# Attention output bias: from a TensorE product per tile to a GpSimd addition behind the first norm

## The reference, cut to what matters

```
for each batch:
  xa = layernorm(x)                        # norm "A"
  x  = x + (attention(q = xa@Wq.T + bq, k = ctx@Wk.T + bk, v = ctx@Wv.T + bv) @ Wo.T + bo)
  x  = x + mixture(layernorm(x))           # norm "R": top-3 of 12 experts, 2 stages of 12 matrices, gelu between
  x  = x + attention(layernorm(x), ctx, ctx)   # norm "C": no projections
  x  = x + moe(layernorm(x))               # norm "D": router over 64 experts, shared expert, routed experts
```

## Time and profile before

| | |
|---|---|
| median of 3 runs | 2767.86 us |
| the profiled execution | 2765.2 us, its span 2763.4 us |
| TensorE (PE) busy | 2616.3 us, 95% of the span |
| VectorE (DVE) busy | 2207.7 us, 80% |
| ScalarE (ACT) busy | 1067.6 us, 39% |
| GpSimd (POOL) busy | 811.1 us, 29% |
| chain that ended last | PE 77%, DVE 12%, issue 4% |

### The profile page before, as it was taken

The page is one execution under the profiler, slowest core; times in us unless marked ns, Lnnn a source line. Parts: engine busy times, 40 slices in busy tenths (PEclk is TensorE's granted clock), DMA queues, the critical chain, the costliest instruction groups (busy, mean ns, idle before and its releaser), DMA issues.

```text
span 2763.4 us, 59981 instructions
## 1 busy us (share of the span) xinstructions
PE 2616.3 (95%) x22949; PEld 2189.8 (79%) x22949; DVE 2207.7 (80%) x6135; ACT 1067.6 (39%) x1622; POOL 811.1 (29%) x829
## 2 busy tenths in 40 slices
PE   3899999999999999999999999999999999985999
PEld 3778788888888888888888888888888888863776
DVE  5677888888888888888888888888888888762554
ACT  3333434444444444433444444444444344322332
POOL 1000133322323232322332232323232232226444
PEclk9999999999999999999999999999999999986999
DMA  7644444444444444443444444444344333245997
GB/s 226 174 141 107 114 127 129 124 109 115 118 118 110 117 112 97 117 118 93 107 112 99 107 117 112 109 112 113 89 106 109 93 98 83 55 87 157 230 234 169
DMA packets 322210, 336.02 MB, mean 122 GB/s; under 512 B 46676, under 2 KB 302751, under 8 KB 321412
## 3 DMA queue, kind: packets, MB, share of 16 engines
q1 hardware_dynamic: 286404, 307.37, 42.8%
q0 software_dynamic: 33792, 18.52, 4.0%
q10 hardware_dynamic: 1728, 6.29, 0.7%
HBM read 191.65 MB, written 221.81 MB: 150 GB/s over the span
## 4 chain that ended last, share of the span: by engine, by line
PE 77%; DVE 12%; issue 4%; DMA 2%; ACT 2%; POOL 2%; SPq 1%; POOLq 0%; ACTq 0%; DVEq 0%
PE mixp L1386 35%; PE attn_out L1320 6%; PE second L1304 5%; DVE nm L978 4%; PE first L1286 4%; DVE hid L1070 3%; PE misc L1254 3%; PE misc L1212 3%; PE mixp L1488 3%; PE misc L1422 2%; PE misc L1331 2%; PE second L1507 2%; PE misc L1461 2%; PE misc L1350 2%; PE first L1443 2%
## 5 line engine op out<-in xcount | busy, mean ns | idle before, releaser
L793 ACT ACTIVATE exps<-second 128x1024 f32<-128x1024 f32 x512 | 525.4, 1026 | 770.9 <-PE second L1304 763.6
L678 POOL DMA_INDIRECT expert_slots<-row_mem,sidx x512 | 510.4, 997 | 820.1 <-PE first L1286 579.1
L1386 PE MATMUL mixp<-w_h,r_part_h 128*128 128x256 f32 x3072 | 664.2, 297 | 2.3 <-DVE r_part_l L888 1.1
L978 DVE TENSOR_REDUCE nm<-first 128x4 f32<-128x1024 f32 x504 | 614.3, 1219 | 24.8 <-PE first L1286 24.2
L1386 PE MATMUL mixp<-w_h,r_part_l 128*128 128x256 f32 x3072 | 609.8, 280 | 0.0
L1386 PE MATMUL mixp<-w_l,r_part_h 128*128 128x256 f32 x3072 | 609.3, 279 | 0.0
L1386 PEld LDWEIGHTS mixp<-w_h,r_part_h 128*128 128x128 f32 x3072 | 467.8, 189 | 43.4 <-issue 2.1
L1386 PEld LDWEIGHTS mixp<-w_l,r_part_h 128*128 128x128 f32 x3072 | 468.8, 188 | 0.0
L1386 PEld LDWEIGHTS mixp<-w_h,r_part_l 128*128 128x128 f32 x3072 | 468.6, 188 | 0.0
L1070 DVE SCALAR_TENSOR_TENSOR x_mem<-mixp,C,x_mem 128x256 f32<-128x256 f32 x768 | 332.6, 477 | 74.5 <-PE mixp L1386 67.5
L1070 DVE SCALAR_TENSOR_TENSOR hid<-mixp,C,hid 128x256 f32<-128x256 f32 x704 | 303.6, 477 | 54.4 <-PE mixp L1386 52.9
(11 more groups left out here) (236 smaller groups left out, 3593.1 us busy)
## 6 DMA issues: line engine op xcount, KB each, us to landing
kst<-k_parts SPq DMA_DIRECT2D x256, 192.0 KB, 4.1
qst<-q_parts SPq DMA_DIRECT2D x256, 192.0 KB, 4.5
q_parts<-nat_h SPq DMA_DIRECT2D x128, 256.0 KB
k_parts<-ctx_part_h SPq DMA_DIRECT2D x64, 256.0 KB, 2.5
k_parts<-nat_h SPq DMA_DIRECT2D x64, 256.0 KB, 5.6
q_parts<-nat_l SPq DMA_DIRECT2D x64, 256.0 KB
exps<-in_wgu SPq DMA_DIRECT2D x30, 384.0 KB, 4.2
expert_slots<-row_mem SPq DMA_DIRECT2D x16, 642.0 KB, 6.5
```

The lines of the kernel that those rows point to most:

```text
L678: pool.e.indirect_dma_start(out=slots_dram, out_offset=bass.IndirectOffsetOnAxis(ap=sidx[b % 2][:, t, k:k + 1], axis=0), in_=row[b % 2][:, ...
L793: act.e.activation(exps[:, j % NU, :, :, :].rearrange("p k t s -> p (k t s)"), second[:, :, :].rearrange("p k s -> p (k s)"), ACT.Exp, sca ...
L978: dve.e.tensor_reduce(nm[u % 2][:, :, 2 * j:2 * j + 2].rearrange("p t k -> p k t"), (mixp_mem if in_mixp(b, kind, j) else first)[:, :, :]. ...
L1386: m = pe.e.matmul(mixp[q % 2][:, t * D:(t + 1) * D], src[i][:, dt, t * P:(t + 1) * P], wmix[n][j][:, l, dt, :], start=(k == 0), stop=(k == ...
```

## The change

GpSimd adds the bias, and all strings are written anew. The parts:

1. At the start TensorE makes one product of `ones` with the whole of `b_rows` (line 1238 of the new kernel), once, and ScalarE copies it into a new tile `bias` (128 x 256): the bias row in each partition. (The rows from 32 on of `ones` are zero, so that b2 does not enter.)
2. A new GpSimd step e of norm A: after VectorE has normalised x of the batch, GpSimd adds `bias` to both tiles of X in one instruction and raises `p_bias`.
3. Step m on TensorE has no bias product, and m on VectorE also waits for `p_bias`.
4. `pw` and `b2_raw`, read only at the start, move into `out_sb`, whose first other write waits for both splits. Semaphore `p_id` becomes the first count of `p_const`.
5. All five strings of `ORDERS` change: GpSimd's by 32 letters e, the others only in order.

```diff
+        bias = sb("bias", (P, D))
-        b_raw = out_sb[0:2, 0, :]
+        b_raw, pw, b2_raw = out_sb[0:2, 0, :], out_sb[0:64, 1, :], out_sb[B2, 1, :]
...
+                elif what == "ln2" and a[0] == "A":
+                    _, b = a
+                    pool.wait_ge(v_norm["A"], 2 * b + 2)
+                    pool.wait_ge(a_b, 3)
+                    pool.e.tensor_tensor(X[b % NXB][:, :, :], X[b % NXB][:, :, :],
+                                         bias[:, :].unsqueeze(1).broadcast_to([P, TILES, D]), ALU.add).then_inc(p_bias, 1)
...
             for c in range(FIRST):
                 load_chunk(2 * FIRST + c)
+            act.wait_ge(t_bo, 2)
+            act.e.copy(bias[:, :], misc[:, 0:D]).then_inc(a_b, 1)
...
                 elif what == "o_proj":
                     b, = a
                     dve.wait_ge(t_o, b + 1)
+                    dve.wait_ge(p_bias, b + 1)
...
             pe.wait_ge(a_id, 1)
+            pe.wait_ge(v_g, 1)
+            pe.wait_ge(v_b, 2)
+            pe.e.matmul(misc[:, 0:D], ones[:, :].broadcast_to([P, P]), b_rows[:, :], start=True, stop=True).then_inc(t_bo, 1)
+            free["misc"] = [(a_b, 3)]
...
                     pe.wait_ge(v_w, 1)
-                    pe.wait_ge(v_b, 1)
                     for t in range(TILES):
                         out = misc[:, t * D:(t + 1) * D]
-                        pe.e.matmul(out, ones[:, :].broadcast_to([P, P]), b_rows[:, :], start=True, stop=False)
                         for i, j in TERMS:
                             for dt in range(DT):
-                                m = pe.e.matmul(out, a_parts[i][:, dt, t * P:(t + 1) * P], wo[j][:, dt, :], start=False,
-                                                stop=(i, j, dt) == (0, 1, DT - 1))
+                                m = pe.e.matmul(out, a_parts[i][:, dt, t * P:(t + 1) * P], wo[j][:, dt, :],
+                                                start=(i, j, dt) == (0, 0, 0), stop=(i, j, dt) == (0, 1, DT - 1))
```

More of the change, by code:

```diff
@@ new lines @@
+        "OTOTOTwcCTDOOTOTdOTOOTOTeTOTOTOTBOTOTTnOOTOTOTwcCTOOTDOTdOTOOTOTeTOTOTOTBOTOTTnOOTOTOTwcCTOOTDOTdOTOOTOTeTOTOT"
+        "OTBOTOTTnOOTOTOTwcCTOOTDOTdOTOOTOTeTOTOTOTBOTOTTnOOTOTOTwcCTOOTDOTdOTOOTOTeTOTOTOTBOTOTTnOOTOTOTwcCTOOTDOTdOTO"
+        "OTOTeTOTOTOTBOTOTTnOOTOTOTwcCTOOTDOTdOTOOTOTeTOTOTOTBOTOTTnOOTOTOTwcCTOOTDOTdOTOOTOTeTOTOTOTBOTOTTnOOTOTOTwcCT"
+        "OOTDOTdOTOOTOTeTOTOTOTBOTOTTnOOTOTOTwcCTOOTDOTdOTOOTOTeTOTOTOTBOTOTTnOOTOTOTwcCTOOTDOTdOTOOTOTeTOTOTOTBOTOTTnO"
+        "OTOTOTwcCTOOTDOTdOTOOTOTeTOTOTOTBOTOTTnOOTOTOTwcCTOOTDOTdOTOOTOTeTOTOTOTBOTOTTnOOTOTOTwcCTOOTDOTdOTOOTOTeTOTOT"
@@ new lines @@
+        "OTBOTOTTnOOTOTOTwcCTOOTDOTdOTOOTOTeTOTOTOTBOTOTTnOOTOTOTwcCTOOTDOTdOTOOTOTeTOTOTOTBOTOTTnOOTOTOTwcCTOOTDOTdOTO"
+        "OTOTeTOTOTOTBOTOTTnOOTOTOTwcCTOOTDOTdOTOOTOTeTOTOTOTBOTOTTnOOTOTOTwcCTOOTDOTdOTOOTOTeTOTOTOTBOTOTTnOOTOTOTwcCT"
+        "OOTDOTdOTOOTOTeTOTOTOTBOTOTTnOOTOTOTwcCTOOTDOTdOTOOTOTeTOTOTOTBOTOTTnOOTOTOTwcCTOOTDOTdOTOOTOTeTOTOTOTBOTOTTnO"
+        "OTOTOTwcCTOOTDOTdOTOOTOTeTOTOTOTBOTOTTnOOTOTOTwcCTOOTDOTdOTOOTOTeTOTOTOTBOTOTTnOOTOTOTwcCTOOTDOTdOTOOTOTeTOTOT"
+        "OTBOTOTTnOOTOTOTwcCTOOTDOTdOTOOTOTeTOTOTOTBOTOTTnOTOOTOTwCOTOTDOOTTOOTOTTOTOTOTBOTOTnTTwTTCTDOOTOOTTOTTOTTOTTT"
@@ new lines @@
+        "QtPfQQsRRvFPQGQhKQRRiQlQQPQRRQpQQPRRrckQtyQQQFPfQGQsRRvQQhKPRRiQlQQQRRPQQpQQPRRrckQtQyQQFPfQGQsRRvQQhKRRPiQQlQ"
+        "QPRRQQpQQPRRrckQtQyQQFPfQGQsRRvQQhKRRPiQQlQQPRRQQpQQPRRrckQtQyQQFPfQGQsRRvQQhKRRPiQQlQQPRRQQpQQPRRrckQtQyQQFPf"
+        "QGQsRRvQQhKRRPiQQlQQPRRQQpQQPRRrckQtQyQQFPfQGQsRRvQQhKRRPiQQlQQPRRQQpQQPRRrckQtQyQQFPfQGQsRRvQQhKRRPiQQlQQPRRQ"
+        "QpQQPRRrckQtQyQQFPfQGQsRRvQQhKRRPiQQlQQPRRQQpQQPRRrckQtQyQQFPfQGQsRRvQQhKRRPiQQlQQPRRQQpQQPRRrckQtQyQQFPfQGQsR"
+        "RvQQhKRRPiQQlQQPRRQQpQQPRRrckQtQyQQFPfQGQsRRvQQhKRRPiQQlQQPRRQQpQQPRRrckQtQyQQFPfQGQsRRvQQhKRRPiQQlQQPRRQQpQQP"
@@ new lines @@
+        "RRrckQtQyQQFPfQGQsRRvQQhKRRPiQQlQQPRRQQpQQPRRrckQtQyQQFPfQGQsRRvQQhKRRPiQQlQQPRRQQpQQPRRrckQtQyQQFPfQGQsRRvQQh"
+        "KRRPiQQlQQPRRQQpQQPRRrckQtQyQQFPfQGQsRRvQQhKRRPiQQlQQPRRQQpQQPRRrckQtQyQQFPfQGQsRRvQQhKRRPiQQlQQPRRQQpQQPRRrck"
+        "QtQyQQFPfQGQsRRvQQhKRRPiQQlQQPRRQQpQQPRRrckQtQyQQFPfQGQsRRvQQhKRRPiQQlQQPRRQQpQQPRRrckQtQyQQFPfQGQsRRvQQhKRRPi"
+        "QQlQQPRRQQpQQPRRrckQtQyQQFPfQGQsRRvQQhKRRPiQQlQQPRRQQpQQPRRrckQtQyQQFPfQGQsRRvQQhKRRPiQQlQQPRRQQpQQPRRrckQtQyQ"
+        "QFPfQGQsRRvQQhKRRPiQQlQQPRRQQpQQPRRrckQtQyQQFPfQGQsRRvQQhKRRPiQQlQQPRRQQpQQPRRrckQtQyQQFPfQGQsRRvQQhKRRPiQQlQQ"
@@ new lines @@
+        "LOoOSMOpOqPwrMMOxSMOyMMDMMOEuMOPMdMfOGMMOJevOSMOhMPHMMiSOMMOlMOmOPnMIMLMOoOSMMOpOqPrMwMOxSMOMyMMDMOEuMOPMdMfOG"
+        "MMOeJvOSMhOMPHMMiOSMMOlMOmOPnSMMIMOLoOMMOpOqPrMwMOSxMOMyMDMMEOuMOPMdMfOGMMOeJvOSMhOMPMHMiOSMMOlMOmOPnSMIMMOLoO"
+        "MMOpOqPrMwMOSxMOMyMDMMEOuMOPMdMfOGMMOeJvOSMhOMPMHMiOSMMOlMOmOPnSMIMMOLoOMMOpOqPrMwMOSxMOMyMDMMEOuMOPMdMfOGMMOe"
+        "JvOSMhOMPMHMiOSMMOlMOmOPnSMIMMOLoOMMOpOqPrMwMOSxMOMyMDMMEOuMOPMdMfOGMMOeJvOSMhOMPMHMiOSMMOlMOmOPnSMIMMOLoOMMOp"
+        "OqPrMwMOSxMOMyMDMMEOuMOPMdMfOGMMOeJvOSMhOMPMHMiOSMMOlMOmOPnSMIMMOLoOMMOpOqPrMwMOSxMOMyMDMMEOuMOPMdMfOGMMOeJvOS"
@@ new lines @@
+        "MhOMPMHMiOSMMOlMOmOPnSMIMMOLoOMMOpOqPrMwMOSxMOMyMDMMEOuMOPMdMfOGMMOeJvOSMhOMPMHMiOSMMOlMOmOPnSMIMMOLoOMMOpOqPr"
+        "MwMOSxMOMyMDMMEOuMOPMdMfOGMMOeJvOSMhOMPMHMiOSMMOlMOmOPnSMIMMOLoOMMOpOqPrMwMOSxMOMyMDMMEOuMOPMdMfOGMMOeJvOSMhOM"
+        "PMHMiOSMMOlMOmOPnSMIMMOLoOMMOpOqPrMwMOSxMOMyMDMMEOuMOPMdMfOGMMOeJvOSMhOMPMHMiOSMMOlMOmOPnSMIMMOLoOMMOpOqPrMwMO"
+        "SxMOMyMDMMEOuMOPMdMfOGMMOeJvOSMhOMPMHMiOSMMOlMOmOPnSMIMMOLoOMMOpOqPrMwMOSxMOMyMDMMEOuMOPMdMfOGMMOeJvOSMhOMPMHM"
+        "iOSMMOlMOmOPnSMIMMOLoOMMOpOqPrMwMOSxMOMyMDMMEOuMOPMdMfOGMMOeJvOSMhOMPMHMiOSMMOlMOmOPnSMIMMOLoOMMOpOqPrMwMOSxMO"
@@ new lines @@
+        "MyMDMMEOuMOPMdMfOGMMOeJvOSMhOMPMHMiOSMMOlMOmOPnSMIMMOLoOMMOpOqPrMwMOSxMOMyMDMMEOuMOPMdMfOGMMOeJvOSMhOMPMHMiOSM"
+        "MOlMOmOPnSMIMMOLoOMMOpOqPrMwMOSxMOMyMDMMEOuMOPMdMfOGMMOeJvOSMhOMPMHMiOSMMOlMOmOPnSMIMMOLoOMMOpOqPrMwMOSxMOMyMD"
+        "MMEOuMOPMdMfOGMMOeJvOSMhOMPMHMiOSMMOlMOmOPnSMIMMOLoOMMOpOqPrMwMOSxMOMyMDMMEOuMOPMdMfOGMMOeJvOSMhOMPMHMiOSMMOlM"
+        "OmOPnSMIMMOLoOMMOpOqPrMwMOSxMOMyMDMMEOuMOPMdMfOGMMOeJvOSMhOMPMHMiOSMMOlMOmOPnSMIMMOLoOMMOpOqPrMwMOSxMOMyMDMMEO"
+        "uMOPMdMfOGMMOeJvOSMhOMPMHMiOSMMOlMOmOPnSMIMMOLoOMMOpOqPrMwMOSxMOMyMDMMEOuMOPMdMfOGMMOeJvOSMhOMPMHMiOSMMOlMOmOP"
@@ new lines @@
+        "QtMyMMuMOQMMOQFRPMfMOQGMQORQJvROSMOQhMMKRPMiMOQSMlOQMQOmQORRPMSMIMQOLMOQMpQORQOqRPMkMOQSMOQtMyMMuMOQMMOQFRPMfM"
+        "OQGMQORQJvROSMOQhMMKRPMiMOQSMlOQMQOmQORRPMSMIMQOLMOQMpQORQOqRPMkMOQSMOQtMyMMuMOQMMOQFRPMfMOQGMQORQJvROSMOQhMMK"
+        "RPMiMOQSMlOQMQOmQORRPMSMIMQOLMOQMpQORQOqRPMkMOQSMOQtMyMMuMOQMMOQFRPMfMOQGMQORQJvROSMOQhMMKRPMiMOQSMlOQMQOmQORR"
+        "PMSMIMQOLMOQMpQORQOqRPMkMOQSMOQtMyMMuMOQMMOQFRPMfMOQGMQORQJvROSMOQhMMKRPMiMOQSMlOQMQOmQORRPMSMIMQOLMOQMpQORQOq"
+        "RPMkMOQSMOQtMyMMuMOQMMOQFRPMfMOQGMQORQJvROSMOQhMMKRPMiMOQSMlOQMQOmQORRPMSMIMQOLMOQMpQORQOqRPMkMOQSMOQtMyMMuMOQ"
@@ L249, in build @@
         b_rows = sb("b_rows", (P, D), F32R)
-        pw_mem = sb("pw", (P, D))
-        pw = pw_mem[0:64, :]
         B2 = slice(64, 64 + 3 * L)
-        b2_raw, b2 = pw_mem[B2, :], b_rows[B2, :]
+        b2 = b_rows[B2, :]
+        bias = sb("bias", (P, D))
         uT = sb("uT", (64, 3 * L))
@@ L377, in build @@
         s_xc = sem("layer_c_sum")
+        p_bias = sem("pool_bias_sum")
         v_mask_bf = sem("vec_mask_bf")
```

127 lines of the change are left out of this document (43 added, 84 removed).

## The result

The changed kernel takes 2846.45 us in the median of 4 runs (2838.02 to 2852.53); the kernel before, beside it, 2766.18 (2763.79 to 2769.37, 4 runs). The ratio is 1.0287, with a 95% interval of 1.0252 to 1.0322. The forecast was 2748. The profiled execution took 2851.79 us, its span is 2850.0.

The account below looks back on a forecast made before the run. TensorE (PE) was taken to set the pace; -0.23 - 0.35 - 0.33 - 0.27 + 0.3 + 0.2 = -0.68 us per period, -20.4 in all from 2765.2: 2744.8, by the median 2748. Range 2717 to 2768.

Parts of the forecast that it names:

- SyncE's queue, N ahead of P: SyncE issues the second N's large DMAs before P's small ones; Q waits +0.2 us per period, bounds 0 and 1.05.
- rival 3: SyncE's queue: P's rows wait behind the spread each period, 1.05 us in place of 0.2; 2776 us, chance 0.12.
- Store j 5 us later: On SyncE, a waits for GpSimd's B and j leaves some 5 us later; cost 0, with 1.5 us to spare.
- Contention of VectorE and GpSimd: VectorE's updates beside GpSimd's addition are not slowed: 0, bounds 0 and 0.1 us per period.
- The products: On TensorE two bias products per batch go: -0.23 us per period, 7.5 us in all 32 batches.
- Q fills J's wait: On TensorE a Q of 0.33 us fills the wait of 0.45 at J: -0.33 us per period.
- S and h ahead of M: On TensorE S and h stand before M, not Q; a transpose takes 0.36 us, not 0.53: -0.35 per period.
- P behind F: VectorE has one update pair less before this P, so TensorE waits less: -0.27 us per period, bound -0.79.
- The wait from l to m: TensorE newly waits at m for VectorE's half of l: +0.3 us per period, bounds 0 and 0.7.
- u ahead of M: On TensorE u moves from before Q to before M: +0.23 us for u, -0.2 at the O, taken as 0.
- The added addition: GpSimd's new bias addition, bounded by 0.7 and 2.6 us each, has nobody waiting for it: cost 0.
- The start: One product more and one ScalarE copy at the start, while TensorE stands idle: cost 0, bounds 0 and 0.5 us once.

Follow-up runs that it names:

- run 8: Kernel before, only SyncE's string edited so the second N is issued ahead of P's small DMAs: 2794.93 us, ratio 1.0098.
- run 6: Changed kernel with SyncE's string of before and GpSimd's copy B moved early, C staying beside x: 2788.82 us, ratio 1.0076.
- run 3: Changed kernel with SyncE's string of the kernel before: 2821.84 us, ratio 1.0205.
- run 9: Kernel before with GpSimd's copy B moved behind ten more O and T: 2785.36 us beside 2785.22, ratio 1.0001.
- run 10: Kernel before with GpSimd's copy B four more O and T later than in run 9: 2886.71 us beside 2783.21, ratio 1.0366.
- run 4: Changed kernel with GpSimd's addition C moved later, no longer beside VectorE's x: 2828.07 us, ratio 1.0219.
- run 1: Kernel before with its order strings kept and only the bias moved to GpSimd, e behind B: 2762.61 us, ratio 0.9985.
- run 2: All five new strings without e, the old bias products staying on TensorE: 2849.82 us, ratio 1.0301.
- run 12: Run 1 with TensorE's Q behind v moved ahead of J: 2775.51 us beside 2785.22, ratio 0.9965.
- run 5: Changed kernel with SyncE's and GpSimd's strings of before, the bias addition behind B: 2777.62 us, ratio 1.0044.
- run 11: Run 6 with GpSimd's addition C two O and a T later: 2821.06 us beside 2785.22, ratio 1.0127; its repeat 2821.89 us, ratio 1.0138.

## Why the prediction was wrong, by its steps

- **SyncE's queue, N ahead of P: the step that failed first.** The working had it right: P's rows 5.9 us after P in place of 4.86, so 1.05. I then took 0.2 in place of that bound, for no row. Measured: 0.95 in the changed kernel, 1.02 alone (run 8). The bound was sharp, partly by luck: the 1.3 us in it stands in none of its rows, and 4.5 and 1.3 make 5.8, which is what Q took behind P (5.80 in the changed kernel, 5.85 in run 8, 4.84 before). That was rival 3, held at 0.12, which names 0.9 us as the point where it decides. The rule cited there, that descriptors start in order within a queue (the Trainium skill, "DMA: Bandwidth & Descriptors", section "Two DMAs through the same engine are not ordered"), fits the runs; how the queue does it they don't show.
- **Store j 5 us later, "0, with 1.5 us to spare": the second.** j left 7.0 us later (20.5 us into the period in place of 13.5). I followed it to the N behind it and to O, which reads what N brings, and stopped there. Behind that N stand P's rows, with another reader: they left at 27.1 us in the period (25.4 with an early B, run 6), and Q, due at 30.1, started at 31.2. Measured +1.14, with what follows 1.5. Runs 3 and 6 differ by B alone and show that it is B. Runs 9 and 10 show in the old order that a late B costs nothing up to a point: with B at 15.2 us no wait, at 20.7 a wait of 2.64. The 1.02 (run 3) and 1.14 at 19.4 belong to the new order, so where the point lies in either is not measured.
- **Contention of VectorE and GpSimd, 0 (bounds 0 and 0.1): the third.** The earlier trace rows showed an update with an operand from PSUM, which indeed isn't slowed. x reads and writes SBUF only, one tensor in and one out; that kind went from 0.41 to 1.38 us. I looked at the added operation, and not at what the new strings put beside the old ones. Measured 0.75 per period (run 4), against 0. The Trainium skill ("SBUF — State Buffer", section "Who interferes with whom") has this: in VectorE's modes with two ports, which `tensor_scalar` can enter, VectorE and GpSimd share one pair of ports, as an exclusive lock held for a whole instruction. The trace agrees: the slow part of x ends 0.15 us behind GpSimd's instruction whatever was left of that.
- **The products, 0.23: right.** 0.236 in the old order (run 1), 0.227 in the new one (m to Q 1.836 us with them in run 2, 1.609 without). What the order does to m is separate: it now follows an O and not an M, its first pair of MATMULs takes 0.33 in place of 0.23, and m takes 1.609 where it takes 1.497 in the old order. And the Q that waits for its rows took part of the gain: it waits 1.03 us in run 2 and 1.14 in the changed kernel.
- **Q fills J's wait, -0.33: right** in place (run 12), a part given back elsewhere.
- **S and h ahead of M, -0.35: too large.** A transpose takes 0.36 us between two Ms, but 0.41 behind an O or Q, in both kernels; the row of 0.36 was of the first kind, the moved steps are of the second. 0.53 to 0.41 for S and 0.585 to 0.41 for h is 0.29.
- **P behind F, -0.27: 0.18** (R to this P takes 1.08 in place of 1.26). But the P at 24 us lost 0.30 (1.288 in place of 0.988) that I did not have. 0.27 of it is the CAST beside an indirect DMA (run 5): the same kind of step as the third.
- **The wait from l to m, +0.3: 0.12**, for VectorE's `a_part_l`. **u ahead of M, +0.23 with -0.2, taken as 0: +0.11** (u, Q and O took 0.99 us together, now 1.11).
- **The added addition, nobody waits: right.** The start, 0: the 2.8 us of the profiled execution are no cost of it that could be told. The first v comes at 125.8 to 127.3 us in kernels with the old start and at 126.0 to 128.6 in those with the new one.

So the new order would have been about even with the old had nothing been lost on the queues: run 5 has a period of 74.87 with 0.46 of it from the lock, run 1 74.54. That the change as it is can be brought there is not shown, since run 11 met another wait.

## What to carry to other kernels

When a string of DMA issues changes, follow each queue past the first reader: every issue behind the delayed one has its own reader, and the one with the least slack decides (here four DMAs of 4 KB behind four of 192 KB). Where the working gives a bound and no row speaks for less, the bound is the value. And when orders move, list which SBUF-only operations of VectorE come to lie beside GpSimd's, its indirect DMAs included, and not only what the new operation lies beside.

## What the runs showed of the hardware

- A 128x256 TENSOR_SCALAR from SBUF to SBUF takes 0.41 us on VectorE, and 0.93 to 1.46 us when it meets a 128x512 TENSOR_TENSOR of GpSimd (in every steady period, lines 672 and 647 alike); it then ends 0.15 us behind GpSimd's. GpSimd's on line 672 takes 1.38 in place of 1.30. VectorE's SCALAR_TENSOR_TENSOR with an operand in PSUM (0.475 us alone, 0.48 beside it) and its TENSOR_REDUCE from PSUM (1.22 and 1.22) did not change. Beside GpSimd's copy B (0.60 us alone, up to 0.75) the same TENSOR_SCALAR took up to 0.83 (runs 5, 6 and 11).
- VectorE's operations can be slowed by GpSimd's indirect DMAs too. A 128x16 CAST went from 0.175 to 0.44 us when it began 0.51 us after the start of one (19 periods), and the second part of x from 0.41 to 0.60 (run 4).
- Four DMAs of 4 KB behind four of 192 KB on one queue: Q starts 5.8 us after P, in place of 4.84, and in single periods 7.2 (run 8).
- A semaphore of TensorE can rise 1.2 us behind the end that the profile shows, with ScalarE waiting for it (run 11 and its repeat; cause open).
